# Expert loops of an audio tower: covered semaphore waits left out, and the outputs' moving operand 128 columns wide in place of 192

## The reference

```python
h = tok_ref(x, ...)                      # strided depthwise conv, group norm, PReLU: (128, 63, 64)
h = h + attn_ref(layernorm(h), ...)      # a selective scan with 16 states
h = h + ffn_ref(layernorm(h), ...)       # 64 experts, the best two for each of 128*63 tokens

def ffn_ref(x, Wr, br, W1, b1, W2, b2):  # D_IN 64, D_HID 128, D_OUT 64
    topk_logits, topk_idx = top_k(xf @ Wr + br, 2)
    gates = softmax(topk_logits, axis=1)
    for e in range(64):
        y = relu(xf @ W1[e] + b1[e]) @ W2[e] + b2[e]
        out = out + combine[:, e:e + 1] * y
```

## Time and profile before

| | us |
|---|---|
| median of 3 runs | 892.1 (891.81 to 896.81) |
| the profiled execution, its own time | 893.91 |
| its span, first to last instruction | 891.9 |
| the expert loops in it, first transpose to last result landed | 613.5 to 799.6 |

### The profile page before, as it was taken

One profiled execution on the slowest core, in us unless ns is written; L12 is line 12 of the kernel. 1 busy time (PEld: TensorE's weight loads), 2 busy tenths in 40 slices (PEclk: granted clock), 3 DMA queues, 4 the chain that ended last, 5 costly groups with the idle time before them and its releaser, 6 DMA issues.

```text
span 891.9 us, 8970 instructions
## 1 busy us (share of the span) xinstructions
PE 482.6 (54%) x2036; PEld 303.3 (34%) x2036; DVE 606.0 (68%) x1015; ACT 334.3 (37%) x589; POOL 553.9 (62%) x398
## 2 busy tenths in 40 slices
PE   4916903366656565675548900004999999970000
PEld 4816901112211121121118900003777767750000
DVE  1389448999999999999974999971444444454111
ACT  2211384565565456454428600001444444430000
POOL 1002104699999999999930027777777077747774
PEclk9965555677986888787785555556999999995555
DMA  6999997000000000000000001203999999961111
GB/s 239 355 122 107 79 53 3 0 0 1 0 0 0 0 0 0 0 0 0 0 0 1 1 6 48 87 25 98 285 292 317 287 286 308 291 198 46 46 56 37
DMA packets 108784, 81.97 MB, mean 92 GB/s; under 512 B 37378, under 2 KB 95362, under 8 KB 108738
## 3 DMA queue, kind: packets, MB, share of 16 engines
q1 hardware_dynamic: 81202, 64.71, 34.2%
q0 software_dynamic: 8064, 8.27, 3.4%
q10 hardware_dynamic: 19472, 8.47, 3.3%
HBM read 58.44 MB, written 31.39 MB: 101 GB/s over the span
## 4 chain that ended last, share of the span: by engine, by line
POOL 35%; PE 23%; DVE 15%; issue 14%; DMA 4%; SPq 3%; ACT 3%; POOLq 1%; DVEq 0%; ACTq 0%
POOL hh_ring L406 14%; PE ps L602 9%; POOL w_ring L391 8%; POOL xt L433 7%; POOL sorted_rows L425 7%; PE ps L591 5%; PE ps L457 3%; DMA x_w<-packed 3%; PE ps L525 2%; SPq L315 2%; PE ps L508 2%; DVE mi L1033 1%; PE ps L581 1%; DVE w_ring L1021 1%; DVE mx L1029 1%
## 5 line engine op out<-in xcount | busy, mean ns | idle before, releaser
L525 PE MATMUL ps<-hh_ring,ident 128*128 128x512 f32 x272 | 177.9, 791 | 154.8 <-POOL hh_ring L406 117.9
L425 POOL DMA_INDIRECT sorted_rows<-xp,slot_i x126 | 122.1, 969 | 113.5 <-DVE slot_i L1059 75.4
L391 POOL TENSOR_TENSOR w_ring<-xt,bc 128x1024 f32<-128x1024 f32 x64 | 154.5, 2415 | 38.8 <-DVE xt L934 38.8
L433 POOL DMA_INDIRECT xt<-expert_out,slot_i x126 | 123.2, 978 | 69.6 <-issue 37.8
L406 POOL TENSOR_TENSOR hh_ring<-hh_ring,bc 128x1024 f32<-128x1024 f32 x63 | 149.1, 2366 | 17.5 <-DVE hh_ring L965 14.6
L525 PEld LDWEIGHTS ps<-hh_ring,ident 128*128 128x128 f32 x272 | 56.9, 229 | 276.5 <-POOL hh_ring L406 185.3
L965 DVE TENSOR_TENSOR_SCAN hh_ring<-ps,w_ring 128x1024 f32<-128x1024 f32 x64 | 145.9, 2279 | 0.1
L602 PE MATMUL ps<-x_w 128*128 128x192 f32 x504 | 116.6, 354 | 0.0
L709 ACT ACTIVATE ps<-dt_t,a_exp 128x1024 f32<-128x1024 f32 x64 | 71.6, 1118 | 78.7 <-DVE w_ring L943 78.7
L713 ACT ACTIVATE ps<-dt_t,a_exp 128x1024 f32<-128x1024 f32 x64 | 71.5, 1117 | 64.3 <-DVE hh_ring L965 64.3
L602 PEld LDWEIGHTS ps<-x_w 128*128 128x128 f32 x504 | 79.5, 191 | 15.3 <-issue 0.5
(11 more groups left out here) (162 smaller groups left out, 625.2 us busy)
## 6 DMA issues: line engine op xcount, KB each, us to landing
x_w<-packed SPq DMA_DIRECT2D x252, 128.5 KB
sorted_rows<-pad_rows SPq DMA_DIRECT2D x2, 4096.0 KB, 18.0
x_w<-sorted_rows SPq DMA_DIRECT2D x32, 256.0 KB
expert_out<-x_w ACTq DMA_DIRECT2D x126, 64.0 KB
packed<-in_L_ffn_W SPq DMA_DIRECT2D x3, 2048.0 KB, 41.6
x_w<-in_x SPq DMA_DIRECT2D x7, 448.0 KB, 9.3
packed<-in_L_ffn_b SPq DMA_DIRECT2D x1, 2048.0 KB, 69.3
sorted_rows<-xp,slot_i POOLq DMA_INDIRECT x126, 2.1
```

The costliest lines, as they stand in the source:

```text
L391: pool.tensor_tensor(w_ring[:, k % 4, :].rearrange("p (d s) -> p d s", s=S), up3[:, bass.ds(c * DC, DC), :], bc[:, k:k + 1, :].broadcast_t ...
L425: pool.indirect_dma_start(out=sorted_rows[k], out_offset=bass.IndirectOffsetOnAxis(ap=slot_i[:, k, l:l + 1], axis=0), in_=xp1[:, l, 0:C], ...
L433: pool.indirect_dma_start(out=y[:, l, :], out_offset=None, in_=expert_out[k], in_offset=bass.IndirectOffsetOnAxis(ap=slot_i[:, k, l:l + 1] ...
L525: ins = pe.matmul(ps[:, i, :], ident[:, :], hh_ring[:, buf, i * BANK:(i + 1) * BANK], start=(k < 0), stop=(k == N - 1), skip_group_check=True)
```

## The change

Two things in one diff. Waits that another wait already covers are left out: on SyncE the wait for `s_yps`, on TensorE those for `s_rTc` in `rows_T` and for `s_reluA` and `s_reluB` in `hidden` (and the wait for rows is made once in four pairs), on ScalarE and VectorE those for `s_win`, `s_hid` and `s_yps` ahead of `xT_copy` and the relus. And OUT is 128 in place of 192: the moving operand of the outputs' matmuls is then columns 128 to 255, W2 and b2, and no longer takes 64 columns of W1 with it. The order of the instructions on each engine stays the same.

```diff
-OUT = 3 * C
+OUT = 2 * C
...
                 if n >= WRING:
-                    sp.wait_ge(s_yps, n - WRING + 1)
                     sp.wait_ge(s_yb, n - WRING + 1)
...
                 u = unit_of(n)
-                pe.wait_ge(s_rows[u % RING], 16 * (u // RING + 1))
-                if n >= 2:
-                    pe.wait_ge(s_rTc, n - 1)
+                if n % PAIRS % UNIT == 0:
+                    pe.wait_ge(s_rows[u % RING], 16 * (u // RING + 1))
...
                 pe.wait_ge(s_rTc, n + 1)
-                if n >= 2:
-                    pe.wait_ge(s_reluA, n - 1)
-                    pe.wait_ge(s_reluB, n - 1)
...
                 act.wait_ge(s_rT, n + 1)
-                if n >= 2:
-                    act.wait_ge(s_hid, n - 1)
                 act.activation(xT_e[:, n % 2, :], ps[:, n % 2, 0:P], ACT.Copy).then_inc(s_rTc, 1)
 
             def relu_A(n):
 
-                act.wait_ge(s_win[n % WRING], 32 * (n // WRING + 1))
                 act.wait_ge(s_hid, n + 1)
...
             def relu_B(n):
 
-                dve.wait_ge(s_win[n % WRING], 32 * (n // WRING + 1))
                 dve.wait_ge(s_hid, n + 1)
-                if n >= 2:
-                    dve.wait_ge(s_yps, n - 1)
```

## The result

The changed kernel takes 907.1 us (median of 4 runs, 905.25 to 919.16), the one before 892.4 (891.81 to 896.81): a ratio of 1.014, with a 95% interval of 1.009 to 1.019. It is slower, by 14.7 us from median to median and by some 13 us by the ratio. Single executions of the kernels with narrow outputs differ by more than those of the others, and the comparison leaves the longest of them out.

The account below looks back on a forecast made before the run. It took TensorE and SyncE, running almost side by side in the expert loops, as the bound. 893.9 - 8.4 of gains + 14 for the clock = 899.5, less 1.8 for the profiled execution: 898 us, range 881 to 935.

Parts of the forecast that it names:

- The beat of TensorE: Expert loops: TensorE's time per pair falls from 1.38 to 1.16 us at full clock, 2.52 to 2.10 at half.
- SyncE as the second bound: Expert loops: SyncE's issuing of loads needs 1.33 us a pair, only 0.05 under TensorE's 1.38, and above 1.16.
- The waits left out: SyncE in the expert loops: one instruction less per load saves 0.055 us, 6.5 us in all, between 2 and 9.
- SyncE's waits for a slot: Expert loops: 4.2 us of waiting for a free slot go at full clock; with slower DMA instructions 0 net, +4 to -4.
- The clock: Expert loops: TensorE starves at loads of expert numbers and falls to half clock in three spells, costing 14 us (2.3 to 28).
- The price of 0.77 us a pair: Expert loops at half clock: TensorE's 2.10 us a pair against SyncE's pace of 1.33, so 0.77 lost a pair.
- the gains: Expert loops: SyncE's saved instruction 6.5 us, slot waits 0, the two loop ends 1.9; sum 8.4 us, bounds 4 to 13.
- The rival in which the clock holds: Expert loops: TensorE stays at full clock and the 8.4 us come through: 884 us, 879 to 888; chance 0.22.
- The one in which it stays down for most of the loops: Expert loops: TensorE stays at half clock; 973 us for all pairs, 930 for half of them; chance 0.23.
- The DMA floor: Expert loops: DMA engines can't bring a pair's weights faster than now, so 892.1 less 0 to 3, 890 us; chance 0.10.

Follow-up runs that it names:

- the two kernels with SyncE relieved: Kernel before with waits left out, 8 expert numbers a load, DMAs of rows on ScalarE, OUT 192 or 160: 884.2 and 883.9 us, ratio 0.988 both.
- waits-only kernel: Kernel before with the waits left out as in the change, OUT kept at 192: 890.2 us, ratio 0.996.
- the other 128-column kernels: OUT 128 with all waits kept (913.1 us); the change with 8 expert numbers a load (894.1 us); the change with 34 matmuls ahead of the loops (910.8 us).
- The kernel with loads of 0.54 us: The change with expert numbers loaded 8 at a time in place of 32: 894.1 us, ratio 0.997.
- the 160-column kernel: The change with OUT 160 in place of 128, waits left out: 893.7 us, ratio 1.000 to the kernel before.
- filler: The change plus one matmul of 128 unread columns ahead of the outputs of each pair: 892.4 us, ratio 0.999 to the kernel before.

## Why the prediction was right

The kernel came out slower by 1.4% where 0.6% was forecast, inside the stated range and for the reason that was given. The forecast of 898 us was within its own 1% of no change, and only 0.38 was given to slower than that; the loss is more than twice the forecast one. By its steps:

- The beat of TensorE: 1.16 and 2.10 us were worked out from the earlier trace rows; 1.17 and 2.09 are there, and an outputs instruction is 275 ns in place of 326.
- SyncE as the second bound: right. TensorE starves at full clock (busy 87%), and the two kernels with SyncE relieved are the fastest.
- The waits left out: 6.5 us forecast, bounds 2 to 9. The waits-only kernel gives 4.1 of medians (894.3 to 890.2). The working has a slip: 4.11 / 4 is 1.03, or 1.04 with the gap to the next, not 1.08, so an instruction's gap is 32 ns and not 38. The traces give 0.045 us a pair: with the DMA of rows four pairs take 4.64 us from start to start in the change (641.48 to 646.12) where they took 4.82, and 119 x 0.045 is 5.4. That a slow DMA instruction is one that the queue is slow to accept no run shows; only its duration is there.
- SyncE's waits for a slot were to go while the clock is full and do (1.1 us from 636.5 to 711); in the spells they come back, 23.9 us in all where they were 4.2.
- The clock. The term was 14 us: three spells of 12 us, each behind a stall. There were three, of 10, 7 and 31, each behind a stall, shorter (1.2 to 1.6 us) than the 2 us foreseen. The number is luck: every load of expert numbers was to bring a stall and every other stall a spell, and only the first fall comes after a load; the stalls that bring no fall were not foreseen, and the other 128-column kernels have four, two and two spells. The kernel with loads of 0.54 us still has its two. From the waits-only kernel to the change, by their ratios, it is 1.8% or 16 us. The price of 0.77 us a pair, 0.37 for a microsecond at half clock, is near what the profiles give: 69 us at half clock and 195.3 of loops for the change, 9 and 177.1 for the 160-column kernel, an estimate of 0.3 for one across two widths.
- What was left out is the start. The prediction said that the way up would be slower but priced it only for later spells. 21 us in place of 6 are 15 more at half clock, by 0.3 to 0.37 about 5 us, and that is half of the 9 us that the forecast (898) is short of. The other half is on the side of the gains: 8.4 us forecast, some 4 measured.
- The rival in which the clock holds is out, in the profiled execution of all four kernels of 128 columns without filler. The one in which it stays down for most of the loops isn't met either: 69 of 195 us. The DMA floor is refuted by the two last kernels: 298 and 316 GB/s with TensorE fed. The rule of the Trainium skill ("TensorE: Matmul & The Clock Gate", on HAM oscillation), by which the clock can fall at every DMA wait between bursts, spoke for the falls. The traces agree in part: in the change three of the five waits of 1.2 us and more were followed by one, and with 192 columns a wait of 1.93 us was not.

## What to carry to other kernels

Where two queues run at nearly the same pace, making TensorE the faster one can make the kernel slower: it starves, behind some of its stalls the clock falls, and then it is the slower one by far. Look at the granted clock before taking useless columns out of a loop that is not bound by TensorE alone; take the time from the queue that starves it first, then narrow. And the more a kernel hangs on the clock, the more its executions differ, so a single trace of it says little of its median.

## What the runs showed of the hardware

- The length of a stall alone doesn't decide whether TensorE's clock falls behind it. In one execution it fell behind stalls of 1.23, 1.36 and 1.57 us and stayed behind 1.22 and 1.61; over the four kernels with 128 columns 10 of 20 stalls of 1.2 us and more were followed by a fall. With 160 columns it stayed behind 1.31, 1.34 and 1.49, with 192 behind 1.93. What decides was not found.
- From the start of the loops the clock took 6 us to rise with 192 columns, 7 with 128 and a matmul of 128 unread ones in each pair, 9 with 160, and 21, 21 and 27 with 128.
- It stayed at 0.50 while TensorE was busy without a pause, or nearly so: for 21 us at the start of the change, for 31 us in its last spell, and for 27 in one with eight numbers a load.
- A load of 32 numbers into SyncE's registers takes 2.04 us, of 8 numbers 0.54: it goes by the number, some 0.065 us each.
- A weight DMA's instruction takes 333 ns on SyncE and at times up to 1592 (1720 in the kernel with eight numbers). What decides that was not tried.
- On one chip the same program took 1058 us in place of 894, with TensorE, VectorE, ScalarE and SyncE standing still together in the loops while GpSimd went on. What is behind it was not tried.
